# Keys stored once per part and queries projected tile by tile in a routed attention layer; a causal mask moved from TensorE to GpSimd

## What is computed

```
scores = jnp.einsum('bhqd,bhkd->bhqk', q, k) / hd ** 0.5
causal = jnp.tril(jnp.ones((S, S), dtype=bool))
scores = jnp.where(causal, scores, -jnp.inf)
attn = jax.nn.softmax(scores, axis=-1)
```

```
tp, ti = jax.lax.top_k(probs, TOP_K)
...
def expert_step(acc, params):
    qw, qb_, kw, kb_, vw, vb_, ow, ob_, g = params
    q = (x @ qw.T + qb_).reshape(B, S, H, Dh).transpose(0, 2, 1, 3)
    k = (x @ kw.T + kb_).reshape(B, S, H, Dh).transpose(0, 2, 1, 3)
    v = (x @ vw.T + vb_).reshape(B, S, H, Dh).transpose(0, 2, 1, 3)
    scores = jnp.einsum('bhqd,bhkd->bhqk', q, k) * scale
    p = jax.nn.softmax(scores, axis=-1)
    o = jnp.einsum('bhqk,bhkd->bhqd', p, v)
    o = o.transpose(0, 2, 1, 3).reshape(B, S, E) @ ow.T + ob_
    return (acc + o * g[..., None], None)
```

## Time and profile before

| | us |
|---|---|
| three executions, median | 3928.61 (3921.69 to 3930.07) |
| the profiled execution | 3943.5, its span 3941.8 |
| causal attention, layer 0 | 791 to 1245 of the span |
| preparation of the routed layer | 2063 to 2308 |
| prologue of the routed loop | 2308 to 2348 |
| routed loop, 35 tiles | 2348 to 3710 |

### The profile page before, as it was taken

One profiled execution on the slowest core, in us unless ns is written; L12 is line 12 of the kernel. 1 busy time (PEld: TensorE's weight loads), 2 busy tenths in 40 slices (PEclk: granted clock), 3 DMA queues, 4 the chain that ended last, 5 costly groups with the idle time before them and its releaser, 6 DMA issues. The chain is left out here.

```text
span 3941.8 us, 128182 instructions
## 1 busy us (share of the span) xinstructions
PE 3228.2 (82%) x54382; PEld 2106.8 (53%) x54382; DVE 2957.4 (75%) x3661; ACT 2518.8 (64%) x4870; POOL 598.6 (15%) x1574
## 2 busy tenths in 40 slices
PE   2999999489997997465855539999999999999638
PEld 1666666235554674122433426666666666666414
DVE  5999999358883113997353449999999999999653
ACT  1899999347776343332211219999999999999622
POOL 0001000021100000563003011111111111111220
PEclk7999999779998998898957759999999999999858
DMA  4000000300000000440005864555554545554410
GB/s 117 9 7 10 8 9 6 100 17 11 9 7 2 22 21 28 171 146 9 1 13 139 246 181 121 123 124 127 125 128 119 128 121 126 123 132 117 106 33 11
DMA packets 206648, 300.80 MB, mean 76 GB/s; under 512 B 91780, under 2 KB 136010, under 8 KB 205030
## 3 DMA queue, kind: packets, MB, share of 16 engines
q1 hardware_dynamic: 199446, 281.40, 27.6%
q10 hardware_dynamic: 2048, 6.29, 0.8%
q0 software_dynamic: 4592, 5.05, 0.5%
HBM read 223.72 MB, written 60.20 MB: 72 GB/s over the span
## 5 line engine op out<-in xcount | busy, mean ns | idle before, releaser
L862 ACT ACTIVATE channels_qk<-psum 128x512 f32<-128x512 f32 x3842 | 2061.4, 595 | 271.0 <-PE psum L705 186.0
L924 DVE TENSOR_REDUCE l2f_chunk_max<-psum 128x2 f32<-128x1024 f32 x1144 | 1327.6, 1220 | 66.2 <-PE psum L680 53.1
L924 DVE TENSOR_REDUCE chunk_max<-psum 128x2 f32<-128x1024 f32 (+2 forms) x832 | 916.9, 1158 | 110.1 <-PE psum L680 59.4
L680 PE MATMUL psum<-l2f_k_parts,l2f_q_parts 48*128 48x512 bf16 x2288 | 698.2, 388 | 42.4 <-DVE l2f_chunk_max L924 30.3
L705 PE MATMUL psum<-l2f_q_parts,l2f_k_parts 51*128 51x128 bf16 x8968 | 711.9, 218 | 1.9 <-ACT channels_qk L862 1.4
L726 PE MATMUL psum<-channels_qk,l2f_v_and_ones 128*9 128x128 f32 x17920 | 697.7, 274 | 12.3 <-issue 12.3
L680 PE MATMUL psum<-k_parts,q_parts 48*128 48x512 bf16 (+3 forms) x1664 | 424.6, 382 | 101.7 <-DMA q_parts<-q_rows_dram 72.0
L705 PEld LDWEIGHTS psum<-l2f_q_parts,l2f_k_parts 51*128 51x128 bf16 x8968 | 483.5, 94 | 38.1 <-ACT channels_qk L862 27.4
L726 PE MATMUL psum<-channels_qk,v_and_ones 128*9 128x128 f32 x12544 | 493.1, 276 | 0.6 <-ACT channels_qk L862 0.5
L705 PE MATMUL psum<-q_parts,k_parts 51*128 51x128 bf16 x6272 | 433.1, 219 | 30.6 <-DMA q_parts<-minus_max_rows 10.4
L726 PEld LDWEIGHTS psum<-channels_qk,l2f_v_and_ones 128*9 128x9 f32 x17920 | 386.4, 90 | 117.3 <-issue 18.2
(11 more groups left out here) (479 smaller groups left out, 3219.5 us busy)
## 6 DMA issues: line engine op xcount, KB each, us to landing
l2f_k_parts<-l2f_k_parts_dram SPq DMA_DIRECT2D x588, 192.0 KB, 3.7
l2f_v_and_ones<-expert_v_dram SPq DMA_DIRECT2D x144, 288.0 KB, 4.0
l1a_bc_rows<-ssm_rows_dram SPq DMA_DIRECT2D x32, 512.0 KB, 4.6
expert_v_dram<-l2f_v_and_ones SPq DMA_DIRECT2D x8, 1152.0 KB, 4.4
channels_qk<-ssm_rows_dram SPq DMA_DIRECT2D x16, 512.0 KB
expert_q_dram<-heads_out SPq DMA_DIRECT2D x8, 1024.0 KB, 7.5
l2f_q_parts<-l2f_gathered_q_parts SPq DMA_DIRECT2D x444, 16.0 KB
k_parts<-k_rows_dram ACTq DMA_DIRECT2D x32, 192.0 KB, 7.3
```

Source lines behind the costliest of these rows:

```text
L680: last = nc.tensor.matmul(c.ps[:, 2 * (n % 2) + j, 0:width], at.q[64 * j:64 * j + ROWS, tile % SLOTS, pair, :], kx(tile)[64 * j:64 * j + R ...
L862: nc.scalar.activation(at.prob[:, s % 4, j, 0:kts, :].rearrange("p k q -> p (k q)"), c.ps[:, ring.bank(i, n), 0:kts * 2 * P], ACT.Exp, sca ...
L924: v.tensor_reduce(at.mx[:, 4 * g + 2 * pp:4 * g + 2 * pp + 2, chunk], c.ps[:, 2 * (n % 2):2 * (n % 2) + 2, 0:span.width(tile, chunk)], X, ...
```

## The change

**Routed layer.** The keys' three parts are stored once each, as 128 rows, and the repeating of rows is done by the load: for each pair and half three DMAs, of 24 rows (the high part three times), 16 rows (the middle part twice) and 8 rows (the low part). The order of the 48 rows changes from channel-major to part-major, and the query loads follow. The queries of all tokens are no longer projected in the preparation: the normalised tokens are stored once, with each expert's query weight and bias; the gather takes tokens, TensorE turns them together with the heads ("turn", step 14), and a matmul with the tile's query weight ("q", step 17) makes the queries; ScalarE adds the bias as it copies. One more load per tile brings that weight. The router drops the table of rows by expert.

**Causal loop.** The matmuls of L714 go. GpSimd zeroes what lies above the diagonal in the exponentials, two selects for each diagonal group, and the value matmuls wait for them.

```
@@ Attention: tensors
-        self.k_dram = nc.dram_tensor(f"{c.layer}k_parts_dram", [8, 2, NPAIR, HD, NR, T], BF16, kind="Internal").ap()
+        self.k_dram = nc.dram_tensor(f"{c.layer}k_parts_dram", [8, 3, 2, NPAIR, HD, T], BF16, kind="Internal").ap()
@@ store_keys
     for which, part in enumerate(parts):
-        n = len(range(NR)[ROWS_OF_K[which]])
-        for j in range(2):
-            eng.dma_start(at.k_dram[bass.ds(e, 1), j, :, :, ROWS_OF_K[which], :].rearrange("e p d n t -> (e p d) n t"),
-                          part[64 * j:64 * j + 64, :].unsqueeze(1).to_broadcast([64, n, T])).then_inc(parts_stored, 16)
+        eng.dma_start(at.k_dram[bass.ds(e, 1), which].rearrange("e j p d t -> (e j p d) t"), part[:, :]).then_inc(parts_stored, 16)
@@ load_keys
     for j in range(2):
-        eng.dma_start(at.kx[64 * j:64 * j + ROWS, buf, pair, :],
-                      at.k_dram[bass.ds(e, 1), j, pair].rearrange("e d r t -> (e d r) t")).then_inc(k_loaded, 16)
+        for which, rows in enumerate(ROWS_OF_K):
+            n = len(range(NR)[rows])
+            at_row = 64 * j + HD * range(NR)[rows][0]
+            eng.dma_start(at.kx[at_row:at_row + HD * n, buf, pair, :], at.k_dram[bass.ds(e, 1), which, j, pair].rearrange("e d t -> (e d) t")
+                          .unsqueeze(0).to_broadcast([n, HD, T])).then_inc(k_loaded, 16)
@@ Ring: side tasks by step
-        if self.routed and s == 12:
-            names.append("q")
-        if self.routed and i > 0 and s in (14, 20):
-            names.append("outT" if s == 14 else "proj")
+        if self.routed and s in (14, 17):
+            names.append("turn" if s == 14 else "q")
+        if self.routed and i > 0 and s == 20:
+            names.append("proj")
@@ attention_loop, SP
+            def load_w_q(tile, e):
+                sp.dma_start(routed.w_q_now[:, tile % 2, :], routed.w_q_dram[bass.ds(e, 1)].rearrange("e p d -> (e p) d")).then_inc(w_q_loaded[tile % 2], 16)
...
                 for g in range(G):
                     load_later_max(i, g)
+                    if g == 0:
+                        load_w_q(i + 2, e)
@@ attention_loop, GpSimd
+            def mask_keys(i, g):
+                s = (g + 1) * span.steps(i) - 1
+                kk = i % 2
+                for j in range(2):
+                    pool.wait_ge(s2_read, ring.read_when(i, ring.place(i, (s, j))))
+                    block = at.prob[:, s % 4, j, kk, :].rearrange("p (a q) -> p a q", a=2)
+                    g_.affine_select(out=block, in_=block, compare_op=ALU.is_ge, fill=0.0, base=0, pattern=[[0, 2], [1, P]],
+                                     channel_multiplier=-1).then_inc(masked, 1)
...
                 for g in range(G):
                     group, tile = first_pass_of(i, g)
+                    if tri is not None:
+                        mask_keys(i, g)
@@ attention_loop, TensorE
-                if diagonal:
-                    kk = len(kts) - 1
-                    for j in halves:
-                        nc.tensor.matmul(c.ps[:, ring.bank(i, place[j]), 2 * kk * P:(2 * kk + 2) * P], c.identb[:, :],
-                                         tri.key[:, :].unsqueeze(1).to_broadcast([P, 2, P]), start=False, stop=True).then_inc(s2_ready, 1)
...
             def weighted_values(s, i):
...
+                if tri is not None and i in kts:
+                    pe.wait_ge(masked, (i * G + g + 1) * 2)
...
+            def project_q(i, n, turned):
                 pe.wait_ge(s2_read, ring.free_when(i, n))
+                pe.wait_ge(s2_read, ring.read_when(i, turned))
+                pe.wait_ge(w_q_loaded[i % 2], (i // 2 + 2) * 16)
+                nc.tensor.matmul(c.ps[:, ring.bank(i, n), 0:P], routed.w_q_now[:, i % 2, 0:P], routed.turned[:, 1, :],
+                                 start=True, stop=True).then_inc(s2_ready, 1)
@@ Routed: what is gathered
-        pool.indirect_dma_start(out=self.q[:, k, :], out_offset=None, in_=self.q_dram[:, :],
+        pool.indirect_dma_start(out=self.q[:, k, :], out_offset=None, in_=self.n_dram[:, :],
@@ l2_router, VectorE, for each of two choices
-                    link(v.tensor_tensor(tmp[:, :, :], choice[:, k], per_column(order[:, :], E), ALU.mult))
-                    link(v.tensor_reduce(where[:, :], tmp[:, :, :], X, ALU.add))
-                    link(v.tensor_scalar(where[:, :], where[:, :], -float(T), float(E * T), ALU.mult, ALU.add))
-                    link(v.tensor_tensor(where[:, :], where[:, :], edge[:, :], ALU.add))
-                    link(v.tensor_scalar(row[:, k, :], where[:, :], index[:, 0:1], None, ALU.add))
```

More of the change, by code:

```diff
@@ L362, in fills @@
         if i == self.tiles:
-            return [(0, 0), (0, 1), "out", "outT", "proj"] if self.routed else ["out"]
+            return [(0, 0), (0, 1), "out", "turn", "proj"] if self.routed else ["out"]
         steps = 4 * self.span.steps(i)
@@ L544, in _ @@
                 first, second = expert(0), expert(1)
+                load_w_q(0, first)
+                load_w_q(1, second)
                 load_group(0, 0, first)
@@ L749, in project @@
                 pe.wait_ge(w_out_loaded, i * 16)
-                nc.tensor.matmul(c.ps[:, ring.bank(i, n), 0:P], routed.outT[:, :], routed.w_out_now[:, :], start=True, stop=True).then_inc(s2_ready, 1)
+                nc.tensor.matmul(c.ps[:, ring.bank(i, n), 0:P], routed.turned[:, 0, :], routed.w_out_now[:, :], start=True, stop=True).then_inc(s2_ready, 1)
             def side_work(i, g, name):
@@ L828, in _ @@
                     pe.wait_ge(routed.gathered[k], 16)
-                    nc.tensor.transpose(c.ps[:, ring.BANK0 + k, 0:P], routed.q[:, k, :], c.ident[:, :]).then_inc(first_q_turned, 1)
+                    nc.tensor.transpose(c.ps[:, ring.BANK0 + k, P:2 * P], routed.q[:, k, :], c.ident[:, :]).then_inc(first_n_turned, 1)
+                for k in range(2):
+                    pe.wait_ge(first_n_copied, k + 1)
+                    pe.wait_ge(w_q_loaded[k], 16)
+                    nc.tensor.matmul(c.ps[:, ring.BANK0 + k, 0:P], routed.w_q_now[:, k, 0:P], routed.turned[:, k, :],
+                                     start=True, stop=True).then_inc(first_q_made, 1)
             for g in range(lead):
@@ L875, in empty @@
                     nc.scalar.activation(at.out[:, :, :], bank.rearrange("p (h n) -> p h n", n=32)[:, :, 0:HD + 1], ACT.Copy).then_inc(s2_read, 1)
-                elif name == "outT":
-                    nc.scalar.activation(routed.outT[:, :], bank[:, 0:P], ACT.Copy).then_inc(s2_read, 1)
+                elif name == "turn":
+                    first, last = 0 if heads else 1, 2 if tokens else 1
+                    nc.scalar.activation(routed.turned[:, first:last, :].rearrange("p a q -> p (a q)"), bank[:, first * P:last * P],
+                                         ACT.Copy).then_inc(s2_read, 1)
                 elif name == "proj":
@@ L882, in empty @@
                     act.wait_ge(qparts_ready, i + 2)
-                    nc.scalar.activation(routed.qT[:, :], bank[:, 0:P], ACT.Copy).then_inc(s2_read, 1)
+                    nc.scalar.activation(routed.qT[:, :], bank[:, 0:P], ACT.Identity, bias=routed.w_q_now[:, i % 2, P:P + 1]).then_inc(s2_read, 1)
                 else:
@@ L897, in _ @@
                 for k in range(2):
-                    act.wait_ge(first_q_turned, k + 1)
+                    act.wait_ge(first_n_turned, k + 1)
+                    nc.scalar.activation(routed.turned[:, k, :], c.ps[:, ring.BANK0 + k, P:2 * P], ACT.Copy).then_inc(first_n_copied, 1)
+                for k in range(2):
+                    act.wait_ge(first_q_made, k + 1)
                     if k:
                         act.wait_ge(qparts_ready, k)
-                    nc.scalar.activation(routed.qT[:, :], c.ps[:, ring.BANK0 + k, 0:P], ACT.Copy).then_inc(first_q_copied, 1)
+                    nc.scalar.activation(routed.qT[:, :], c.ps[:, ring.BANK0 + k, 0:P], ACT.Identity,
+                                         bias=routed.w_q_now[:, k, P:P + 1]).then_inc(first_q_copied, 1)
             for g in range(lead - ring.late):
@@ L911, in _ @@
             if routed:
-                empty("outT", done, 3)
+                empty("turn", done, 3, tokens=False)
                 empty("proj", done, 4)
@@ L2200, in _ @@
                 link(v.tensor_copy(rt.rounds[:, :], many[0:1, 0:1]))
+                link(v.tensor_scalar(row[:, :], edge[:, :], index[:, 0:1], None, ALU.add))
                 link(v.tensor_scalar(first[:, :], first[:, :], float(P), None, ALU.mult))
```

137 lines of the change are left out of this document (68 added, 69 removed).

## The result

The changed kernel takes 4547.56 us (the median of four runs, 4546.91 to 4552.69) against 3929.34 us: a ratio of 1.158, with a 95% interval of 1.1561 to 1.1598, or +618 us. It is slower, as forecast, but by less than the 870 us forecast.

What follows compares the result with a forecast made beforehand. The prediction took the routed loop as PE-bound, then bound by DMA engines carrying the keys. Terms -18, -2.3, -80, +910 and +60 sum to +870 on the 3928.6 us median: 4800 us, range 4000 to 5350.

Steps and rivals of the forecast that it cites:

- the few engines: Routed loop: the key loads run on 3, 2 and 8 DMA engines, so the first engine needs 63 to 72 us a tile.
- 12 us of margin: Routed loop: the SP queue waits 12 us of each 38.9 us tile, too little to hold the added key loads.
- 27 - 8 + 48 x (0.78 to 0.92) + 0.5 = 57 to 64: Routed loop: SP's time per tile in us, with 48 key loads at 0.60 to 0.74 issue plus 0.18 of registers.
- Every load of few rows is dearer: Key loads: few-row loads issue in 0.607 to 0.76 us, against 0.32 for 48 rows; argued against the old issue price.
- I take 65 us a tile: Routed loop: the slower of SP and first DMA engine sets the tile, +26 us over 35 tiles, +910 us.
- Preparation: Layer's preparation: 5.7 MB per expert become 3.2, 24 us become 14, so -80 us, bounds -60 and -95.
- Mask: Causal loop: removing 128 mask matmuls saves 18 us, bounds -24 and +30.
- 64 steps x 0.32: Causal loop: each of 64 diagonal steps loses 0.32 us of mask matmuls, 20 us before DVE takes over a little.
- The new wait, the upper bound: Causal loop: PE waits on two GpSimd selects; expected covered, otherwise up to 0.8 us a step, some 50 us gross.
- Prologue: Prologue before the routed loop: 84 key loads for 28 cost +60 us, bounds +26 and +90.
- Rival 1: Routed loop: SP alone bounds, short loads issue in 0.32 us on all engines, 43.5 us a tile, 4017 us; 17%.
- Rival 3: Routed loop: idling PE falls to 1.2 GHz, its 38.2 us of work a tile take 76, 5190 us; 7%.

Runs made afterwards that it cites:

- experiment 3: Changed kernel with two pairs side by side in key storage, 24 key loads a tile in place of 48, same bytes on the same engines: 4373.67 us, ratio 1.1097.
- experiment 5: Changed kernel with key parts still stored once, 48 loads a tile of 24, 16 and 8 neighbouring rows without repeat dimension: 4023.2 us, ratio 1.0257.
- experiment 1: Changed kernel with the keys stored and loaded as before the change, everything else of the change kept: 3916.26 us, ratio 0.9936.
- experiment 2: Kernel before the change with each 48-row key load cut into three of 16 rows, from the same storage: 4282.94 us, ratio 1.086.

## Why the prediction was right, and where it failed

**Direction: right. Which limit decides: wrong.** The prediction had two limits above the 38.9 us of a tile, SP at 57 to 64 us and the few engines at 63 to 72, and let the engines decide. Both exist, in the other order: the engines at 51.3 us (experiment 3), SP at 57.6. The SP queue's 12 us of margin went, and SP became the bound. Its sum, "27 - 8 + 48 x (0.78 to 0.92) + 0.5 = 57 to 64", came out: 48 key issues with their registers take 0.78 us each, 37 in all, and the rest 20. It was the low end, because a third of the loads, those of 8 rows, cost 0.29. What TensorE waited for was not keys and queries, as the prediction had it, but values (471 us) and rows of maxima (104 us at its weight loads). That the total still fell inside the range owes something to luck: the two limits lie within 7 us of each other.

**"Every load of few rows is dearer": wrong.** This was a reading of the earlier trace rows; experiment 5 has 8 rows at 277 ns. Two of those dear rows, L480 and L489, have a second dimension in the destination that the source lacks; in L255 the source has a repeat dimension. This likeness to the dear loads of the change is argued; no run changes any of the three. The sum came out since two thirds of the new loads had a repeat dimension, and that is luck.

**"I take 65 us a tile": too high.** The term from the engines, 272 packets at 0.20 to 0.23 us, was mis-sized: a packet took 0.159 us, and experiment 3 has 51.3 us for the whole term. So SP's count was the slower of the two, +19 us a tile and not +26: 35 x 7.4 = 260 us, against 252 by which the whole forecast was too high; the other terms cancel. (L255 is also not "the one load whose outermost dimension is 3": the maxima loads are 3x2x128 in the order printed above. They carry 1.5 KB each, so the sum doesn't change.)

**Preparation.** -80 forecast, -93 to -100 measured. At 12.0 to 12.6 us an expert in the steady part it was below the 13.4 of the sum and the 14 taken. The form of the stores counts too: the keys now go out as whole 128-row stores, and in experiment 3, where the same bytes went out as six stores of 64 rows, an expert took 17.9 to 18.8 us from the third store on.

```profile
q1 hardware_dynamic: 14641, 23.23, 80.9%
...
l2f_k_parts_dram<-l2f_part_hi SPq DMA_DIRECT2D x4, 512.0 KB
```

The engines are busy at 0.81 of the time, with 512 KB a part; 3.2 MB in 12.3 us is 260 GB/s, above the 241 of the earlier trace rows. Of the gain, some 78 us are the keys' (232 us in experiment 1, 154 here), the rest the queries'.

**Mask.** -18 forecast, -8 to -10 measured, by the selects and by no mask alike. What failed is "64 steps x 0.32": half of that time or more went to ScalarE's wait for the second pass. The prediction named VectorE as what takes over, and it is busy 216 of 250 us; that it is the cause is argued. The new wait, the upper bound, cost nothing. **Prologue**: +60 against +54.

**Rival 1**, SP alone at the old price, had 43.5 us a tile and 4017 us, and experiment 5 measured 43.5 us and 4023 us. That is luck in part: experiment 2 is the rival's own case, 48 issues at the old price with both register instructions, and took 47.5 us; experiment 5 made up for the held issues by fewer register instructions. **Rival 3**: the clock was granted 0.84 in the loop, a mean of its two levels of 1.2 and 2.4 GHz, and did not decide, since TensorE's 41.4 us busy a tile stood far below 57.6. In one tile it was 0.89 for 16 us, 13.7 of them busy, 0.59 for the 13 us from 3026 on in which TensorE sat idle, 0.81 for the next 17 us and 0.95 for the 26 after.

## What to carry to other kernels

Count what a queue has left (its waits), then multiply its issues by their own duration, form by form, before trading bytes stored for DMAs issued: here 2.5 MB less to store per expert, 1.5 of them keys, gave back 93 to 100 us once, and the keys' way of loading cost 653 us in a loop that issued three loads for one (160 to 300 us of it by the number of issues alone, experiments 5 and 2). A repeat written as an extra dimension of the source cost 752 ns an issue where neighbouring rows cost 303, for 24 rows, so it pays to order the data so that a plain run of rows does the repeating, even at the price of storing one part twice. Where one queue issues several DMAs, look at the outermost dimension too: 8 in place of 3 and 2 took a tile from 51.3 to 40.5 us once the issues were halved.

## What the runs showed that I had not expected

The issue time goes neither by rows nor by engines: 8, 16, 24, 32 and 48 neighbouring rows all issue in 277 to 376 ns at the median, with or without a second dimension that both sides have (two pairs a load: 310 ns). And an expert's start in the preparation can come 30 us late in one execution and not in the next, on identical code, while the kernel's time moves by less. In the first profile, while GpSimd issued its scatters of the query list one after the other, the matmuls of L167 started 1.4 to 2.8 us apart from 2090 to 2113, and VectorE stood for 30 us; why, no run shows.
